# Both expert stages of the fourth layer as one run of 78 tiles, with the first weights brought by transfer and held stationary

## The reference

```python
# in _L3_attn_ref (the "mix" experts)
for e in range(E):
    h = jax.nn.silu(flat @ W1[e]) * (flat @ W3[e])          # 128 -> 256, twice
    out = out + cw[:, e:e + 1] * (h @ W2[e])                # 256 -> 128
# in _L3_ffn_ref (the "ffn" experts)
def _swiglu(h):
    x_glu = jnp.minimum(h[..., ::2], LIMIT)                 # LIMIT = 7.0
    x_lin = jnp.clip(h[..., 1::2], -LIMIT, LIMIT)
    return x_glu * jax.nn.sigmoid(ALPHA * x_glu) * (x_lin + 1.0)
def body(acc, ew):
    w1, b1, w2, b2, we = ew
    h = _swiglu(t @ w1 + b1)                                # 128 -> 512
    y = h @ w2 + b2                                         # 256 -> 128
    return (acc + we[:, None] * y, None)
```

## Time and profile before

| what | value |
|---|---|
| median of 3 runs | 960.28 us (958.65 to 960.83) |
| profiled execution | 963.37 us, its span 962.1 us |
| mean granted TensorE clock | 0.844 |
| PE busy | 696.2 us (72%), 4255 instructions |
| DVE busy | 589.9 us (61%) |
| ACT busy | 395.6 us (41%) |
| POOL busy | 285.3 us (30%) |
| DMA | 72.90 MB, mean 76 GB/s |

### The profile page before, as it was taken

One profiled execution on the slowest core, in us unless ns is written; L12 is line 12 of the kernel. 1 busy time (PEld: TensorE's weight loads), 2 busy tenths in 40 slices (PEclk: granted clock), 3 DMA queues, 4 the chain that ended last, 5 costly groups with the idle time before them and its releaser, 6 DMA issues. The chain is left out here.

```text
span 962.1 us, 14376 instructions
## 1 busy us (share of the span) xinstructions
PE 696.2 (72%) x4255; PEld 518.5 (54%) x4255; DVE 589.9 (61%) x1621; ACT 395.6 (41%) x952; POOL 285.3 (30%) x300
## 2 busy tenths in 40 slices
PE   4889967752788379229986797989964429979980
PEld 3889834642667358228865474656543215546550
DVE  5665568528688612386667556879844328864944
ACT  3101324433744223135443335767761114446652
POOL 2243134440000164300000002445411754453551
PEclk9999958856699779668997798999985759998995
DMA  9991001211100150318007321222100212214214
GB/s 281 228 289 51 1 19 46 57 46 31 44 1 1 9 47 8 102 60 350 1 1 186 104 61 33 73 73 72 48 3 22 64 48 57 62 47 140 75 56 134
DMA packets 79561, 72.90 MB, mean 76 GB/s; under 512 B 9617, under 2 KB 73884, under 8 KB 78976
## 3 DMA queue, kind: packets, MB, share of 16 engines
q1 hardware_dynamic: 58880, 53.41, 20.1%
q0 software_dynamic: 7072, 12.38, 5.2%
q10 hardware_dynamic: 13536, 6.21, 2.7%
HBM read 42.83 MB, written 27.42 MB: 73 GB/s over the span
## 5 line engine op out<-in xcount | busy, mean ns | idle before, releaser
L1069 POOL DMA_INDIRECT ys<-work,back_to x101 | 101.2, 1002 | 115.9 <-issue 52.2
L2656 DVE TENSOR_REDUCE work<-banks 128x2 f32<-128x512 f32 x128 | 83.2, 681 | 15.6 <-PE banks L2647 14.8
L995 PE MATMUL banks<-weights,work 128*128 x156 | 88.6, 653 | 1.6 <-issue 1.6
L978 PEld LDWEIGHTS banks<-consts,work 128*128 128x128 f32 x156 | 18.8, 147 | 90.6 <-issue 54.3
L978 PE MATMUL banks<-consts,work 128*128 128x128 f32 x156 | 33.7, 299 | 35.2 <-DVE work L3357 15.2
L2647 PE MATMUL banks<-work 96*128 96x256 bf16 x256 | 49.7, 279 | 8.1 <-DVE work L2656 4.8
L988 PE MATMUL banks<-weights,work 128*128 x312 | 52.7, 293 | 2.6 <-issue 2.3
L789 POOL DMA_INDIRECT xs<-t,idx x48 | 49.2, 1025 | 14.8 <-issue 14.0
L1349 POOL DMA_INDIRECT g<-rows,back_to x16 | 15.3, 958 | 122.5 <-DVE back_to L2067 117.9
L3060 PE MATMUL banks<-work 99*128 99x256 bf16 x256 | 48.9, 277 | 0.9 <-issue 0.9
L988 PEld LDWEIGHTS banks<-weights,work 128*128 128x128 f32 x312 | 42.9, 199 | 5.0 <-issue 3.8
(11 more groups left out here) (497 smaller groups left out, 1914.0 us busy)
## 6 DMA issues: line engine op xcount, KB each, us to landing
weights<-in_w SPq DMA_DIRECT2D x1, 6668.0 KB, 19.6
xs<-zero SPq DMA_DIRECT2D x2, 2580.0 KB, 31.7
work<-xs ACTq DMA_DIRECT2D x78, 64.5 KB
weights<-in_w SPq DMA_DIRECT2D x1, 4569.5 KB, 33.3
weights<-in_r SPq DMA_DIRECT2D x1, 2950.5 KB, 26.2
weights<-in_w SPq DMA_DIRECT2D x1, 2124.5 KB, 12.2
ys<-zero SPq DMA_DIRECT2D x1, 2048.0 KB, 27.7
g<-ys SPq DMA_DIRECT2D x8, 256.0 KB, 3.3
```

Of the source, the lines that this page charges most:

```text
L978: ins = pe.transpose(bank(mb + m % 4)[:, 128 * f:128 * f + 128], self.ha[m % 4][:, f * 128:(f + 1) * 128], self.c["ident"])
L995: pe.matmul(bank(mb + n % 4, F), self.hT[n % 4], self.w1[:, bass.ds(off[n] * (F // 128), F)], start=True, stop=True).then_inc(*self.prod1. ...
L1069: g.indirect_dma_start(self.ys[:, :], bass.IndirectOffsetOnAxis(ap=self.n.back_to[:, k:k + 1], axis=0), self.answer(n), None, bounds_check ...
L2656: v.tensor_reduce(self.mxb[:, 2 * h:2 * h + 2], self.n.bank(bank).rearrange("p (r n) -> p r n", r=2), AX, ALU.max, negate=True).then_inc(* ...
```

## The change

The two classes of experts are replaced by one, `TwinExperts`, a single run of 78 tiles: tiles 0 to 38 are the ffn tiles and 39 to 77 the mix tiles.

- **First weights.** They are no longer kept in SBUF. A transfer on SP fetches the expert's 128x512 weights (for ffn with four more columns that hold the bias) for each tile, five tiles ahead, into one of six buffers. The rows are brought by SP too, four tiles ahead.
- **First product.** Four products with a 128x128 piece of the weights stationary and the turned rows moving, 128 wide. The hidden values come out already turned, so the two turns (978) and ACT's copy (1029) are gone.
- **Ffn hidden values.** The bias is now one number per partition. ACT takes out two of the four pieces with the bias (`ffn_linear`), DVE then takes out the other two with bias and limit (`glu`) and limits the linear part (`clipped`); silu on ACT and the product on DVE follow. There is no DVE instruction 512 wide any more.
- **Order within a step.** PE's step t does the second product of tile t-3, turns the rows of tile t+1, then does the first product of tile t. DVE's step t does the product of tile t-2, then the ffn limits of tile t, then takes out tile t-4.
- **Around it.** 32 answer buffers; `FfnGate` and the ffn `Back` start at step 49; `Load3` brings 4096 + 4096 columns of weights and 4096 columns of bias fewer.

```diff
--- before.py
+++ after.py
@@ -107,9 +107,9 @@
 R2 = [("bv", 128)]
 W3 = [("q", 128), ("k", 128), ("v", 128), ("gate", 128), ("ssm", 256), ("ssm_out", 128), ("attn_out", 128),
       ("halt", 2), ("router", 8), ("gate_w", 8), ("ln_g", 1), ("ln_b", 1), ("norm", 1), ("conv_b", 1), ("ln2_g", 1), ("ln2_b", 1),
-      ("w13", 4096), ("w2", 2048), ("mlp1", 4096), ("mlp2", 2048)]
+      ("w2", 2048), ("mlp2", 2048)]
 R3 = [("ls1", 128), ("ls2", 128), ("halt_b", 2), ("step_b", 3), ("conv_w", 512),
-      ("gate_b", 8), ("mlp1_b", 4096), ("mlp2_b", 1024)]
+      ("gate_b", 8), ("mlp2_b", 1024)]
 SAME_PE = (
...
@@ -175,6 +175,10 @@
         self.w2, self.r2 = w2.on(w2s, 0), r2.on(w2s, w2.width)
         a = w3.width + r3.width
         self.beyond = wts[:, a:a + TOK + NT]
+        a += TOK + NT
+        self.expert_w = [wts[:, a + 516 * i:a + 516 * i + 516] for i in range(6)]
+        a += 6 * 516
+        self.answers = [wts[:, a + C * i:a + C * i + C] for i in range(32)]
         self.stats = sb("stats", [P, NT, 6])
         self.v = [sb(f"small{i}", [P, NT]) for i in range(15)]
         self.k8 = [sb(f"byexpert{i}", [P, NT, E]) for i in range(8)]
...
+class TwinExperts(Stage):
...
+    FFN, TILES, RETURNS = 39, 78, 32
     ALPHA = 1.702
...
+    def offset(self, eng, n):
+        route, k = (1, n) if self.ffn(n) else (0, n - self.FFN)
+        return eng.value_load(self.n.routes[route][2][0:1, k:k + 1], min_val=0, max_val=7 * 128)
+    def sp(self):
+        n, sp = self.n, self.sync
+        for s in self.at[0]:
+            sp.wait_ge(*s)
+        held = len(n.expert_w)
+        def rows(t):
+            if t in (0, self.FFN):
+                for s in self.sources[t > 0]:
+                    sp.wait_ge(*s)
+            xs, r = (n.xs[3], t) if self.ffn(t) else (n.xs[2], t - self.FFN)
+            if t >= 4:
+                sp.wait_ge(*self.turned.at(t - 4))
+                sp.wait_ge(*self.to.at(t - 4))
+            sp.dma_start(self.rows[t % 4], xs[r * P:(r + 1) * P, :]).then_inc(*self.row_in[t % 4].up())
+        def weights(t):
+            if t == self.FFN:
+                for s in self.at[1]:
+                    sp.wait_ge(*s)
+            off = self.offset(sp, t)
+            if t >= held:
+                last = t - held
+                sp.wait_ge(*(self.glu.at(last) if self.ffn(last) else self.prod1.at(last)))
+            src, width = (n.ins["mlp1"], 516) if self.ffn(t) else (n.ins["w13"], 512)
+            sp.dma_start(n.expert_w[t % held][:, 0:width], src[bass.ds(off, P), :]).then_inc(*self.weights_in[t % held].up())
+        for t in range(held - 1):
+            weights(t)
+        for t in range(4):
+            rows(t)
+        for t in range(self.TILES):
+            if t + held - 1 < self.TILES:
+                weights(t + held - 1)
+            if t + 4 < self.TILES:
+                rows(t + 4)
+            yield
+    def pe(self):
+        n, pe, bank, w = self.n, self.tensor, self.n.bank, self.n.expert_w
+        off = {}
+        def turn(t):
+            if t < self.TILES:
+                if t >= 2:
+                    pe.wait_ge(*self.xT.at(t - 2))
+                pe.wait_ge(*self.row_in[t % 4].at(t // 4))
+                pe.transpose(bank(t % 2, 128), self.rows[t % 4][:, 0:C], self.c["ident"]).then_inc(*self.turned.up())
+        turn(0)
+        for t in range(self.TILES + 3):
+            m = t - 3
+            if t < self.TILES:
+                off[t] = self.offset(pe, t)
+            if m >= 0:
+                w2 = n.w3["mlp2" if self.ffn(m) else "w2"]
+                pe.wait_ge(*self.a.at(m))
+                if m >= 2:
+                    pe.wait_ge(*self.y.at(m - 2))
+                for f in range(2):
+                    ins = pe.matmul(bank(6 + m % 2, 128), self.ab[m % 4][:, f * 128:(f + 1) * 128],
+                                    w2[:, bass.ds(off[m] * 2 + 128 * f, 128)], start=(f == 0), stop=(f == 1))
+                ins.then_inc(*self.prod2.up())
+            turn(t + 1)
+            if t < self.TILES:
+                if t >= 4:
+                    pe.wait_ge(*(self.glu.at(t - 4) if self.ffn(t - 4) else self.a.at(t - 4)))
+                pe.wait_ge(*self.weights_in[t % len(w)].at(t // len(w)))
+                pe.wait_ge(*self.xT.at(t))
+                for f in range(4):
+                    ins = pe.matmul(self.mid(t)[:, f * 128:(f + 1) * 128], w[t % len(w)][:, f * 128:(f + 1) * 128], self.hT[t % 4],
+                                    start=True, stop=True)
+                ins.then_inc(*self.prod1.up())
+            yield
+    def act(self):
+        n, a, w3 = self.n, self.scalar, self.n.w3
+        def turned(t):
+            if t < self.TILES:
+                gain, bias = (w3["norm"], 0.0) if self.ffn(t) else (w3["ln2_g"], w3["ln2_b"])
+                if t >= 4:
+                    a.wait_ge(*self.prod1.at(t - 4))
+                a.wait_ge(*self.turned.at(t))
+                a.activation(self.hT[t % 4], n.bank(t % 2, 128), ACT.Identity, scale=gain, bias=bias).then_inc(*self.xT.up())
+                a.activation(n.back_to[:, t:t + 1], self.rows[t % 4][:, C:C + 1], ACT.Copy).then_inc(*self.to.up())
+        turned(0)
+        a.wait_ge(*self.A.now())
+        a.activation(n.scrap[:, :], n.scrap[:, :], ACT.Silu).then_inc(*self.A.up())
+        for t in range(self.TILES + 1):
+            turned(t + 1)
+            u = t % 4
+            if self.ffn(t):
+                if t >= 4:
+                    a.wait_ge(*self.a.at(t - 4))
+                a.wait_ge(*self.prod1.at(t))
+                for f in (2, 3):
+                    ins = a.activation(self.second[u][:, (f - 2) * 128:(f - 1) * 128], self.mid(t)[:, f * 128:(f + 1) * 128],
+                                       ACT.Identity, bias=n.expert_w[t % len(n.expert_w)][:, 512 + f:513 + f])
+                ins.then_inc(*self.linear.up())
+            m = t - 1
+            if m >= 0 and self.ffn(m):
+                if m >= 4:
+                    a.wait_ge(*self.a.at(m - 4))
+                a.wait_ge(*self.glu.at(m))
+                a.activation(self.sg[m % 4], self.first[m % 4], ACT.Silu, scale=self.ALPHA).then_inc(*self.silu.up())
+            if self.FFN <= t < self.TILES:
+                a.wait_ge(*self.a.at(t - 4))
+                a.wait_ge(*self.prod1.at(t))
+                a.activation(self.sg[u], self.mid(t)[:, 0:256], ACT.Silu).then_inc(*self.silu.up())
+            yield
+    def dve(self):
+        n, v = self.n, self.vector
+        off = {}
+        for t in range(self.TILES + 4):
+            m, u = t - 2, (t - 2) % 4
+            if self.ffn(t):
+                off[t] = self.offset(v, t)
+            if 0 <= m < self.TILES:
+                if m >= 4:
+                    v.wait_ge(*self.prod2.at(m - 4))
+                v.wait_ge(*self.silu.at(m))
+                if self.ffn(m):
+                    v.wait_ge(*self.clipped.at(m))
+                    v.scalar_tensor_tensor(out=self.ab[u], in0=self.second[u], scalar=1.0, in1=self.sg[u], op0=ALU.add,
+                                           op1=ALU.mult).then_inc(*self.a.up())
+                else:
+                    v.tensor_tensor(self.ab[u], self.sg[u], self.mid(m)[:, 256:512], ALU.mult).then_inc(*self.a.up())
+            u = t % 4
+            if self.ffn(t):
+                v.wait_ge(*self.linear.at(t))
+                for f in range(2):
+                    ins = v.tensor_scalar(self.first[u][:, f * 128:(f + 1) * 128], self.mid(t)[:, f * 128:(f + 1) * 128],
+                                          n.expert_w[t % len(n.expert_w)][:, 512 + f:513 + f], 7.0, ALU.add, ALU.min)
+                ins.then_inc(*self.glu.up())
+                v.tensor_scalar(self.second[u], self.second[u], 7.0, -7.0, ALU.min, ALU.max).then_inc(*self.clipped.up())
+            m = t - 4
+            if m >= 0:
+                if m % 4 == 0 and m >= self.RETURNS:
+                    v.wait_ge(*self.returned((m - self.RETURNS) // 4))
+                v.wait_ge(*self.prod2.at(m))
+                if self.ffn(m):
+                    v.scalar_tensor_tensor(out=self.answer(m), in0=n.bank(6 + m % 2, 128), scalar=1.0 / self.ALPHA,
+                                           in1=n.r3["mlp2_b"][:, bass.ds(off[m], 128)], op0=ALU.mult, op1=ALU.add).then_inc(*self.y.up())
+                else:
+                    v.tensor_copy(self.answer(m), n.bank(6 + m % 2, 128)).then_inc(*self.y.up())
+            yield
...
@@ -3515,17 +3472,14 @@
     n.run(mix)
     sent2 = Dispatch(n, "2", n.t1_ids, n.xs[2], 0, 2, [n.cleared[2].at(0), mix.placed.at(1)], ids=n.t1_ids[:, :, C])
     n.run(sent2)
-    ffn = FfnExperts(n, n.xs[3], n.ys[3], [sent3.done(), mix.placed.at(1)], n.w3["mlp1"], n.w3["mlp2"], 1)
-    n.run(ffn)
+    experts = TwinExperts(n, [route.tiles.at(0)], [mix.tiles.at(0)], [sent3.done(), mix.placed.at(1)], [sent2.done()])
     xt = n.xT[:, :, :].rearrange("p b n -> p (b n)")[:, 0:NT * C]
```

(12 more changed lines are left out.)

294 lines of the change are left out of this document (58 added, 236 removed).

## The result

The changed kernel takes 1062.58 us (median; 1054.05 to 1070.33, 4 runs), the kernel before 960.56 beside it: a ratio of 1.101 [1.096, 1.107]. The median lies 30 us above the 1032 of the prediction and 8 us above the upper end of its range; the forecast of a slower kernel was right. The profiled execution took 1054.05 us, its span 1052.7, at a mean granted clock of 0.798 against 0.844. Two groups of the page tell most of it. PE, the busiest engine, has 22 us more busy time than before, and 104 us of idle time stand ahead of its second product (3249), 70 of them ended by DVE's taking out (3333).

The account below looks back on a forecast made before the run. The prediction took a circular wait through PE, ACT and DVE to bound the changed ffn tiles: +75 us there, +71 with the small terms, on 963.4 gives 1035, less 3.1 for the median: 1032 us, range 993 to 1055.

Parts of the forecast that it names:

- the mechanism: Ffn tiles: PE's second product waits for DVE's taking out, queued behind limits needing the youngest first product; 3.6 to 5.0 us a tile.
- I take seven tenths of the time at half, 4.6 us a tile: Ffn tiles 8 to 38: mostly half clock, between ends 3.6 and 5.0 us; thirty tiles cost +75 us (+45 to +87).
- a rival in the prediction: Ffn tiles: PE's clock stays full, 3.6 us a tile, +35 to +38 us in all, 995 to 998 us; chance 0.23.
- Handover (2): From ffn tile 38 to mix tile 0: 10.0 us becomes a period of 1.6 in one run, -8.4 us.
- the ring: Ffn tiles: circular wait through PE, ACT and DVE, so successive tiles don't overlap; 3.6 us at full clock, 5.0 at half.
- The fetch (6): Mix part: ffn answers fetched only at the step where DVE first wants them, partly covered by four banks; +3 us (0 to +4).
- The half clock at the start of the mix tiles (5): First mix tiles: begin at half clock, three tiles 1.3 longer, less what their start pays now; +3 us (0 to +5).
- The faster pace without the gate (3): Mix tiles without `FfnGate` beside them: PE's 1.63 us becomes 1.43 for 19 tiles, -3.8 us.
- Start (1): Ffn stage start, the slow stretch from 754 to 790 us: one tile lost, +3 us (0 to +10).
- SP and the transfers (7): Both tile parts: SP's issuing is hidden and DMA has room, 0 us; +2 if SP's cover ran out in the mix part.
- below every period: POOL's returns take 1.29 us each, less than any tile's period, so they cost 0 us.
- The rival without a ring, 936 or 947 us,: Ffn tiles: stages overlap and busy-time savings arrive, -25 us, or -13 if a two-tile product chain binds; chance 0.07.

Follow-up runs that it names:

- e1: Changed kernel with DVE taking out tile t-4 ahead of the ffn limits of tile t: 971.68 us, ratio 1.006 to the kernel before.
- e2: Changed kernel, list order kept, with three banks instead of two for second products and three instead of four for first products: 970.11 us, ratio 1.006.
- second pair: Changed kernel and kernel before, both run again unedited on another chip: 1014.08 us (ratio 1.100) and 922.31 us.
- e7: As e1, with the ffn answers fetched from step 46 instead of 49: 919.72 us, ratio 0.998 to the kernel before.
- first pair: Changed kernel and kernel before as first measured beside each other, no edit: 1062.58 and 960.56 us, ratio 1.101.
- e9: As e7, but only 256 of the 512 weight columns brought for a mix tile: 918.59 us, ratio 0.997 to the kernel before.
- e5: As e1, with PE's second product of tile t-4 instead of t-3 and the ffn answers fetched from step 46: 915.43 us, ratio 0.9945.
- e10: As e5, with the ffn answers fetched at step 53 and `FfnGate` from step 56: 913.1 us, ratio 0.986 to the kernel before.
- e11: As e1, with the ffn answers fetched at step 50 and `FfnGate` from step 53: 917.53 us, ratio 0.998 to the kernel before.

## Why the prediction had the mechanism right and the size wrong

**The mechanism held.** PE idle 2.0 us in each ffn tile, right ahead of 3249, released by 3333; DVE waiting at 3323 for 3287, that for 3259: all as said, and e1 and e2, at 1.006, show that nearly all of the loss goes with it. This was not luck: the chain was read from the order of the two lists, against the busy times, which fell for DVE.

**The step that failed is a size: "I take seven tenths of the time at half, 4.6 us a tile".** The span grew by 90.6 us where the sum had 71. Of the 20 us between them 9 lie in these tiles, 4 at the handover and 6 in the mix part. Between tiles 8 and 38 the clock was full for 20.4 of 147.0 us, 5.4 tiles; 24.6 of 30 ran at half. And a turn took 5.20 at half and 3.7 at full instead of 5.0 and 3.6: with the hand-overs PE's part was 3.24 instead of 3.07 and DVE's 1.30 instead of 1.09, ACT's 0.66 instead of 0.72 (the terms for PE at half add up to 2.95, not the 2.97 written). Together 4.90 a tile, +84.2 instead of +75; by an estimate from these lengths each of the two, share and length, made about half of the 9 us. In the second pair a tile took 4.71, with two thirds of the tiles at half, about the share forecast, and the part still came to +79.3: the share isn't a constant of the kernel.

The other 11 us between 1032 and the median are no term of the sum. The median was put 3.1 us below the profiled run, as for the kernel before; it lies 8.5 above it. The longer runs had a lower clock (0.791 and 0.789, against 0.798 in the profiled one), which fits a larger share of half clock, but they have no profile that would show it.

The Trainium skill, "TensorE: Matmul & The Clock Gate", section "Loop structure matters more than you think", stood as a rival in the prediction. It has copies out of PSUM leave the clock full, in a loop whose next products follow immediately. Here they did not follow: PE waited 2.0 us in each tile for ACT's and DVE's work, and the granted clock was 0.50 for 58 us in one piece, with PE busy 34.5 of them. The forecast was right to follow instead.

**Small terms.** Handover (2): -4.8, not -8.4, because mix tile 0 is still inside the ring: it waits for the taking out that stands behind the limits of tile 38 (947.17 above). Without the ring, e1 has 1.7 us there, the -8.3 of the forecast. The fetch (6), +3 with the four banks as cover: the wait of 6.05 us ran through to PE as 5.29, and mix tile 12 began 7 us late against the kernel before; e7 takes most of it back. The half clock at the start of the mix tiles (5), +3, did not come: mix tile 5 began 8.6 us after mix tile 0, against 9.4 before. The faster pace without the gate (3), -3.8, does not show either: the last seven mix tiles took 12.5 us against 11.8, though single ones follow at 1.45. Start (1): +3.3 in the first pair, as said, but partly by luck: from tile 0 to tile 8, through the slow stretch, the change took 55.0 us, and e1 and e2, which have no ring, took 53.4 and 50.9, so one tile lost to the ring can't be told from what that stretch does. In the second pair, where no slow stretch hides it, the ring bites from tile 5 on and the term is +7.5.

**Terms at nothing.** SP and the transfers (7): no cost shows (e1, and e9 for the mix part). POOL was rightly at nothing under the ring, but my reason, "below every period", was too short: it is below each tile's period, not below the sum. Its 32 scatters and 39 ffn returns are one queue of 71 x 1.29 = 92 us.

**The rival without a ring, 936 or 947 us,** would have been wrong too. With the ring gone, e1 stands at 1.006. Its tile of 2.12 us is the chain of the product over two tiles (on one chip 2.09 in e7 and 1.82 in e5, which differ in that chain alone), and the 13 to 25 us that the rival promised went into the late fetch and, where that is early, into POOL's queue (e5: 8 us gained by the tiles, 10.4 lost at one wait). With the later `FfnGate` a larger part of the gain seems to reach the end (0.986 in e10, 0.9945 in e5, on different chips).

**Open:** what sets the share of half clock; how much of e10's lead over e11 is PE's slack; what makes the stretch from 754 to 790 slow on one chip.

## What to carry to other kernels

Before adding up busy times, write down for each wait how many tiles back it reaches, and what is queued ahead of the instruction that answers it: a taking out placed behind a wait for the youngest tile turns a double buffer into none, and the full length of the path becomes the period. A ring that leaves PE idle can also cost clock, here 35 of 84 us. And sum each queue over the whole section, not per tile: once the ring was gone, the queue of scatters and returns held up the ffn answers (10.4 us in e5) and was busy 142 of 159 us in e10, so the next gain had to respect it.
